# A graph network on one core: scores, value products and logits side by side, V copied by VectorE, loads reordered, last softmax by thirds

## The reference, cut to what matters

```
h   = relu(layernorm(x))                          # before M, and again before G
q,k,v = h@Wq+bq, h@Wk+bk, h@Wv+bv                 # 6 heads of 64
p   = softmax(q k^T / 8 + (0 where adj, else -9e15))
x1  = x + (p v)@Wf + bf                           # M and its residual

h   = relu(layernorm(x1))
hw  = h@W (12 heads of 32);  t = tanh(hw)
z   = leaky(t.w_src + (t.w_dst)^T), -999 where there is no edge
f   = elu(softmax(z) @ hw + b)
g   = sigmoid(h@H_w^T + H_b)
x2  = x1 + g*f + (1-g)*h                          # G and its residual
```

## Time and profile before

| | us |
|---|---|
| median of 3 runs | 2048.41 (2048.01 to 2048.42) |
| the profiled execution's own time | 2048.47 |
| its span in the profile | 2046.4 |
| PE busy in the span | 1979.5 (97%) |
| ACT busy | 1953.5 (95%) |
| DVE busy | 1813.4 (89%) |
| POOL busy | 1629.2 (80%) |
| mean granted clock of TensorE | 0.988 |

### The profile page before, as it was taken

How to read it: one execution, slowest core, us unless ns; L and a number is a source line. 1 busy time by engine, 2 the same in 40 slices (tenths; PEclk the granted TensorE clock), 3 DMA queues, 4 the chain that set the end, 5 groups by cost and what they waited for, 6 DMA issues and landing times.

```text
span 2046.4 us, 58352 instructions
## 1 busy us (share of the span) xinstructions
PE 1979.5 (97%) x19596; PEld 1845.0 (90%) x19596; DVE 1813.4 (89%) x4117; ACT 1953.5 (95%) x6800; POOL 1629.2 (80%) x2859
## 2 busy tenths in 40 slices
PE   4999999999999999999999999999999999999983
PEld 4899999999999999999999999999999999999972
DVE  4689999999999999999999999999999999999884
ACT  3799999999999999999999999999999999999995
POOL 3478888888888888888888888878888878888864
PEclk9999999999999999999999999999999999999995
DMA  5012223323323222223432222222222222221122
GB/s 170 12 46 67 70 60 79 86 68 91 86 65 83 53 51 57 56 50 82 122 99 58 53 52 60 50 53 61 50 52 61 50 54 60 50 52 49 39 47 50
DMA packets 309330, 130.62 MB, mean 64 GB/s; under 512 B 229547, under 2 KB 308782, under 8 KB 309038
## 3 DMA queue, kind: packets, MB, share of 16 engines
q1 hardware_dynamic: 309038, 126.90, 24.8%
HBM read 69.42 MB, written 57.41 MB: 62 GB/s over the span
## 4 chain that ended last, share of the span: by engine, by line
ACT 49%; DVE 37%; PE 5%; issue 4%; POOL 2%; DMA 1%; DVEq 1%; SPq 1%; POOLq 0%
ACT LG L506 27%; ACT LA L500 14%; DVE LG L636 11%; DVE neg_max L640 10%; DVE LA L613 9%; DVE stats L617 3%; ACT cT_hi L558 2%; ACT QKT L514 2%; ACT v L566 2%; PE psum L731 2%; DVE rdenG L632 1%; DVE rden L611 1%; ACT sdT L572 1%; PE psum L741 1%; DMA xin<-x 1%
## 5 line engine op out<-in xcount | busy, mean ns | idle before, releaser
L506 ACT ACTIVATE LG<-LG,neg_max 128x128 f32<-128x128 f32 x1536 | 595.4, 392 | 15.9 <-DVE neg_max L640 8.8
L500 ACT ACTIVATE LA<-LA,neg_max 128x128 f32<-128x128 f32 x768 | 297.9, 400 | 0.0
L506 ACT ACTIVATION_READ_ACCUMULATOR LG<-LG,neg_max 128x1 f32 x1536 | 291.9, 190 | 0.0
L430 POOL TENSOR_TENSOR prod<-th,vec 128x384 f32<-128x384 f32 x256 | 254.3, 1017 | 6.9 <-ACT th L543 6.9
L636 DVE COPY_PREDICATED_SCALAR LG<-no_edge,no_edge_score 128x1536 f32 x128 | 245.5, 1918 | 7.4 <-ACT LG L525 7.3
L640 DVE TENSOR_REDUCE neg_max<-LG 128x12 f32<-128x1536 f32 x128 | 224.4, 1753 | 13.8
L741 PE MATMUL psum<-hT_hi,qk_hi 128*128 128x256 f32 x1152 | 212.4, 292 | 8.5 <-DVE hT_lo L655 8.5
L613 DVE TENSOR_TENSOR LA<-LA,rden 128x768 f32<-128x768 f32 x128 | 199.0, 1555 | 4.4
L741 PE MATMUL psum<-hT_hi,qk_lo 128*128 128x256 f32 x1152 | 200.8, 282 | 0.0
L741 PE MATMUL psum<-hT_lo,qk_hi 128*128 128x256 f32 x1152 | 200.6, 282 | 0.0
L525 ACT ACTIVATE LG<-psum 128x1536 f32<-128x1536 f32 x128 | 186.4, 1457 | 2.3 <-PE psum L814 2.3
(11 more groups left out here) (121 smaller groups left out, 6201.5 us busy)
## 6 DMA issues: line engine op xcount, KB each, us to landing
context<-gcT SPq DMA_DIRECT2D x512, 48.0 KB, 2.1
back<-context SPq DMA_DIRECT2D x128, 192.0 KB, 2.5
xin<-x SPq DMA_DIRECT2D x64, 192.0 KB, 2.4
x_mid<-x SPq DMA_DIRECT2D x64, 192.0 KB, 2.4
xin<-x_mid SPq DMA_DIRECT2D x64, 192.0 KB, 2.4
out<-x SPq DMA_DIRECT2D x64, 192.0 KB, 2.3
ahead<-stage SPq DMA_DIRECT2D x16, 288.0 KB, 3.5
stage<-w_qk SPq DMA_DIRECT2D x12, 192.0 KB, 3.6
```

The lines of the kernel that those rows point to most:

```text
L430: last = pool.tensor_tensor(prod[:, i, :], th[:], vec[:, r.pair(k - 2), 2 + i, :], ALU.mult)
L500: last = act.activation(head, head, ACT.Exp, scale=-1.0, bias=neg_max[:, 0, h:h + 1], accum_out=rsum[:, h:h + 1])
L506: last = act.activation(head, head, ACT.Exp, bias=neg_max[:, 1, a:a + 1], accum_out=den[:, a:a + 1])
```

## The change

- PE's order in a step becomes: queries and keys (one third), V, LA transposes, LG transposes 0-3 and 8-11, sdT, LG 4-7, then scores, value products, logits, graph value products, then bias row, gate, h, hM and hG transposes, queries and keys (two thirds), O. Banks are dealt out anew.
- DVE copies V (`tensor_copy`), not ACT. ACT, DVE and POOL have new orders too, and other offsets between engines and graphs: steps run over k = -3 .. 136, and POOL, for one, does the gate layernorm for graph k-4 where it was k-1.
- The first pieces of the weights come in another order (`PIECES`), pieces 9 to 14, the graphs 4 to 7 and others are issued from the steps (`LOAD_STEP`), the splits move (`SPLIT_STEPS`), the bias setup too. POOL's `setup(-2)` for hb_row stays at -2, the first step with POOL work.
- The last graph's prelu, mask and maximum are done in three parts of four heads each; the exponentials of a part wait for that part's maximum. ACT's exponentials now stand as heads 8-11 at the end of a step and 0-3 and 4-7 in the next.
- SP: context, stores and loads at other offsets, the adjacency load last in a step.

The diff, cut to its core (of PE's order the new one, without the lines that it replaces):

```diff
-FIRST_STEP, STEPS_BEHIND = -7, 5
+FIRST_STEP, STEPS_BEHIND = -3, 9
...
-        PIECES = [("c00", 0, QK_ORDER[0] * 128, 128), ("c02", 0, QK_ORDER[2] * 128, 128),
-                  ("c01", 0, QK_ORDER[1] * 128, 128), ("c10", 0, QK_ORDER[3] * 128, 128),
-                  ("c12", 0, QK_ORDER[5] * 128, 128), ("c11", 0, QK_ORDER[4] * 128, 128),
+        PIECES = [("c01", 0, QK_ORDER[1] * 128, 128), ("c00", 0, QK_ORDER[0] * 128, 128),
+                  ("c02", 0, QK_ORDER[2] * 128, 128), ("c11", 0, QK_ORDER[4] * 128, 128),
                   ("V", 1, 0, COLS), ("V", 1, COLS, COLS),
+                  ("c10", 0, QK_ORDER[3] * 128, 128), ("c12", 0, QK_ORDER[5] * 128, 128),
                   ("O", 1, D, COLS), ("O", 1, D + COLS, COLS),
                   ("gate", 2, D, COLS), ("gate", 2, D + COLS, COLS),
                   ("h", 2, 0, COLS), ("h", 2, COLS, COLS)]
         READY = {name: n + 1 for n, (name, _, _, _) in enumerate(PIECES)}
-        SPLIT_STEPS = {-4: range(0, 3), -3: range(3, 6), -2: range(6, 8), -1: range(8, 11), 0: range(11, 14)}
+        LOAD_STEP = [-1, -1, -1, 0, 0, 0]
+        SPLIT_STEPS = {-2: range(0, 3), -1: range(3, 6), 0: range(6, 8), 1: range(8, 11), 2: range(11, 14)}
...
-        sdT_ps = psum[0:ROWS, 7, 512 - N:512].bitcast(BF16).rearrange("p (i n) -> p i n", i=2)
+        sdT_ps = psum[0:ROWS, 3, 512 - N:512].bitcast(BF16).rearrange("p (i n) -> p i n", i=2)
...
+                for m in range(8, len(PIECES)):
+                    if k == LOAD_STEP[m - 8]:
+                        load_piece(m)
+                for i in range(4, SLOTS):
+                    if k == max(i + -4, -1):
+                        load_x(x, i, i)
+                if k == 1:
+                    load_adj(HALF_SLOTS, 1)
+                    sp.dma_start(wf_stage[1], w_vf[1][:, D:2 * D].rearrange("(c p) n -> p c n", p=128)).then_inc(s["wf_in1"], 16)
+                    sp.dma_start(vec[:, 1, :, :], vecs[1].partition_broadcast(128)).then_inc(s["vec_in1"], 16)
...
                 if k == -2:
                     pool.wait_ge(s["hb_in"], 16)
                     head_bias()
-                if k == -1:
+                if k == 3:
...
+                if r.has(k - 6):
+                    if k - 6 < ALL - 1:
+                        act.wait_ge(s["z_max"], r.done(k - 6))
+                    else:
+                        act.wait_ge(s["last_max0"], 1)
+                    graph_exps(range(0, 4)).then_inc(s["z_exp0"], 1)
...
+                if r.has(k - 5):
+                    act.wait_ge(s["z_ps"], r.done(k - 5))
+                    if k - 5 < ALL - 1:
+                        act.activation(LG[:].rearrange("p (e n) -> p e n", e=3), banks(0, 3), ACT.Prelu, alpha=SLOPE).then_inc(s["z_leaky"], 1)
+                    else:
+                        for q in range(QUADS):
+                            act.activation(LG[:, q * 4 * N:(q + 1) * 4 * N], bank(0 + q), ACT.Prelu, alpha=SLOPE).then_inc(s["z_leaky" if q == QUADS - 1 else f"last_leaky{q}"], 1)
...
-                    act.wait_ge(s["z_max"], r.done(k - 3))
+                    if k - 5 < ALL - 1:
+                        act.wait_ge(s["z_max"], r.done(k - 5))
+                    else:
+                        act.wait_ge(s["last_max2"], 1)
                     graph_exps(range(8, 12)).then_inc(s["z_exp2"], 1)
...
+                        dve.wait_ge(s["masks"], r.done(k - 6))
+                        dve.copy_predicated(LG_heads, no_edge[:, (k - 6) % 2, :].unsqueeze(1).broadcast_to([128, GH, N]),
+                                            no_edge_score[:].unsqueeze(2).broadcast_to([128, GH, N])).then_inc(s["z_masked"], 1)
+                        dve.wait_ge(s["z_masked"], r.done(k - 6))
+                        dve.wait_ge(s["z_masked"], r.done(k - 6))
+                        dve.tensor_reduce(neg_max[:, 1, :], LG_heads, AX.X, ALU.max, negate=True).then_inc(s["z_max"], 1)
+                    else:
+                        dve.wait_ge(s["masks"], r.done(k - 6))
+                        for q in range(QUADS):
+                            heads = slice(4 * q, 4 * q + 4)
+                            if q == QUADS - 1:
+                                dve.wait_ge(s["z_leaky"], ALL)
+                            else:
+                                dve.wait_ge(s[f"last_leaky{q}"], 1)
+                            dve.copy_predicated(LG_heads[:, heads, :], no_edge[:, (k - 6) % 2, :].unsqueeze(1).broadcast_to([128, 4, N]),
+                                                no_edge_score[:].unsqueeze(2).broadcast_to([128, 4, N])).then_inc(s["last_masked"], 1)
+                            dve.wait_ge(s["last_masked"], q + 1)
+                            dve.tensor_reduce(neg_max[:, 1, heads], LG_heads[:, heads, :], AX.X, ALU.max, negate=True).then_inc(s[f"last_max{q}"], 1)
...
+                    dve.wait_ge(s["m_v"], r.done(k))
+                    dve.tensor_copy(v[:, (k) % 4, :], bank(2)[:, 0:D]).then_inc(s["m_val"], 1)
...
+                if r.has(k - 1):
+                    if (k - 1) % 2 == 0:
+                        for i in range(3):
+                            pe.wait_ge(s[f"qk{i}"], r.done(k))
+                    wait_latest(pe, r, ("g_lo", k - 4), ("s_max", k - 2))
+                    wait_latest(pe, r, ("g_haug", k - 5), ("s_max", k - 2))
+                    for h in range(MH):
+                        i = place_of(h)
+                        rows = slice(64 * (h % 2), 64 * (h % 2) + 64)
+                        at = slice((k - 1) % 4 * N, ((k - 1) % 4 + 1) * N)
+                        last = pe.matmul(bank(6 + i // KC)[:, (i % KC) * N:(i % KC + 1) * N],
+                                         QKT[rows, h // 2, at], QKT[rows, KC + h // 2, at], start=True, stop=True)
+                    last.then_inc(s["s_ps"], 1)
+                if r.has(k - 2):
+                    pe.wait_ge(s["pt"], r.done(k - 2))
+                    pe.wait_ge(s["m_val"], r.done(k - 2))
+                    wait_latest(pe, r, ("pt", k - 2), ("qk2", k), ("cT_lo", k - 3))
                     for h in range(MH):
                         i = place_of(h)
                         for e in range(2):
                             rows = slice(h % 2 * MD + e * GD, h % 2 * MD + (e + 1) * GD)
+                            last = pe.matmul(bank(5)[rows, h // 2 * N:(h // 2 + 1) * N], v[:, (k - 2) % 4, h * MD + e * GD:h * MD + (e + 1) * GD],
                                              PTA[:, i * N:(i + 1) * N], start=True, stop=True)
                     last.then_inc(s["c_ps"], 1)
+                if r.has(k - 5):
+                    pe.wait_ge(s["g_sdR"], r.done(k - 5))
+                    wait_latest(pe, r, ("gpt2", k - 6), ("x1", k - 3), ("z_leaky", k - 6))
+                    wait_latest(pe, r, ("gpt0", k - 6), ("m_lo", k + 2), ("z_leaky", k - 6))
+                    wait_latest(pe, r, ("gpt1", k - 6), ("m_val", k), ("qk0", k), ("z_leaky", k - 6))
                     for q in range(QUADS):
                         rows = slice(q * GROUP, (q + 1) * GROUP)
+                        last = pe.matmul(bank(0 + q), sdT[rows, (k - 5) % 2, :], sdR[rows, (k - 5) % 2, :, :].rearrange("p a n -> p (a n)"), start=True, stop=True)
                     last.then_inc(s["z_ps"], 1)
...
+                if r.has(k - 6):
+                    pe.wait_ge(s["gpt0"], r.done(k - 6))
+                    pe.wait_ge(s["gpt1"], r.done(k - 6))
+                    pe.wait_ge(s["gpt2"], r.done(k - 6))
+                    pe.wait_ge(s["g_haug"], r.done(k - 6))
+                    wait_latest(pe, r, ("g_sdR", k - 5), ("gc", k - 7))
                     for a in range(GH):
                         rows = slice(a % 4 * GD, (a % 4 + 1) * GD)
+                        last = pe.matmul(bank(3)[rows, a // 4 * N:(a // 4 + 1) * N], hv[:, (k - 6) % 2, a * GD:(a + 1) * GD],
                                          PTG[:, a // 4, (a % 4) * N:(a % 4 + 1) * N], start=True, stop=True)
                     last.then_inc(s["gc_ps"], 1)
+                if r.has(k - 4):
+                    weights("gate", k - 4)
+                    pe.wait_ge(s["g_lo"], r.done(k - 4))
+                    wait_latest(pe, r, ("pt", k - 2), ("qk1", k + 1), ("g_gate", k - 5))
+                    pe.matmul(bank(4)[:, 0:D], ones[ROWS:128, :], hb3[ROWS:128, r.pair(k - 4), :], start=True, stop=False)
+                    nodes_times(bank(4)[:, 0:D], g_hi, g_lo, hg_hi, hg_lo, D, begun=True).then_inc(s["g_gate_ps"], 1)
```

More of the change, by code:

```diff
@@ L398, in step @@
             def step(r, k):
[L399 to L406, removed]
@@ L417, in step @@
-                if r.has(k - 4):
-                    pool.wait_ge(s["g_gate"], r.done(k - 4))
-                    pool.tensor_scalar(gate[:, (k - 4) % HELD, :], gate[:, (k - 4) % HELD, :], 0.5, 0.5, ALU.mult, ALU.add).then_inc(s["g_sigmoid"], 1)
+                split_ahead(k)
+                if r.has(k - 6):
+                    pool.wait_ge(s["g_th"], r.done(k - 6))
+                    for i in range(2):
```

(30 more changed lines are left out.)

518 lines of the change are left out of this document (225 added, 293 removed).

## The result

The changed kernel takes 2077.13 us (median of 4 runs, 2075.77 to 2077.97) where the one before, run beside it, takes 2048.21 (2047.48 to 2048.42). The ratio is 1.0141, 95% interval 1.013 to 1.0153: slower, by 29 us. The prediction was 2074, with the right sign and, in the main, the right cause.

The account below looks back on a forecast made before the run. PE's full step was taken to bound the kernel: 2048.4 us, plus 0.20 x 122 steps = 24.4, plus 1.3 (-2 early steps, -1 filling, +5 draining, -0.7 last graph), gives 2074 us; range 2062 to 2088, 8 in 10 within 2039 to 2093.

Parts of the forecast that it names:

- PE's sum sets the pace: Steady middle: PE has no gap, so its step of 15.28 us is the period; the change makes it 15.48.
- rival (b): Steady middle: DVE becomes the bound, its waits exceeding its room; 15.63 us a step, 2092 us; chance 0.13.
- Changes of shape inside the tiled run: PE's tiled run: going between two tiled shapes costs as much as to or from the full array, 0.10 to 0.11 us.
- lone bias row: PE, behind the graph value products: bias row loses its cover beside the logits; its 384 columns cost 0.16 us alone.
- (a): PE's tiled run: shape changes inside it are free; net -0.14 us a step, 2033 us; chance 0.18.
- (c): PE's tiled run: new shape changes cost 0.05 us each, net about 0.02 a step, 2052 us; chance 0.09.
- Net per step: PE's steady step: 0.50 us new less 0.30 gone, net +0.20, over 122 steps +24.4 us.
- Filling: Start: POOL's hb_row wait delays the first query product to about 27.0 us; first graph value product earlier, net -1 us.
- Draining: After the last query product: first of six outstanding logit products comes later, against thinner steps; +5 us, bounds -3 and +12.
- the one that I said would stay: Draining loop: gate product waits for the logits before it, and these for th, prod, sd and its parts on POOL.
- Thirds: Last graph: prelu, mask and maximum in thirds gain two thirds of the prelu less four instruction starts, -0.7 us.
- DVE's room, 0.65 less 0.5: DVE's steady step: 14.83 us of work leaves 0.65 us under 15.48; a 0.5 us wait for hT_hi fits.

Follow-up runs that it names:

- Experiment 5: Kernel before, with V copied by DVE instead of ACT, between the second y and sdR: 2048.7 us, ratio 0.9999.
- Experiment 1: Changed kernel with graph value products ahead of the logits in PE's order, the bias row beside the logits: 2033.6 us, ratio 0.9923.
- experiment 2: Changed kernel with only the gate's bias row moved from behind the graph value products to beside the logits: 2046.8 us, ratio 0.9992.
- experiment 4: Changed kernel with POOL's wait for hb_row moved from step -2 to step 0: 2069.7 us, ratio 1.0107.
- experiment 6: Changed kernel without the last graph's split, prelu, mask and maximum of all twelve heads at once: 2075.82 us (one run).
- experiment 7: Changed kernel with the last graph's exponentials in the order of their maxima, heads 0-3, 4-7, 8-11: 2075.34 us (one run).
- experiment 3: Kernel before, with V copied by DVE instead of ACT, behind gT_lo and ahead of hv and y: 2121.09 us, ratio 1.035.

## Why the prediction was right

- **PE's sum sets the pace: right.** Experiment 5 shows it for the kernel before, experiments 1 and 2 for the changed one, whose period follows PE's order to the hundredth. In its middle PE waited for nobody; rival (b) did not come about. DVE's wait for hT_hi is there in 37 of 96 steps.
- **Changes of shape inside the tiled run: right.** Value products to logits cost 0.11 (0.11 predicted), logits to graph value products and those to the bias row 0.11 each and 0.02 for the slow start. The lone bias row costs 0.16 of columns. Rivals (a) and (c) fall. Experiment 1 does land at (a)'s numbers, 15.10 and 2033.6 against 15.14 and 2033, but by avoiding the changes that (a) took to be free; the likeness is chance.
- **Net per step: 0.20 predicted, 0.227 measured** (15.507 - 15.280). The rest, 0.03, is the V product. Behind the tiled run its later trios ran at 0.52 (1208.26 to 1208.78); behind queries and keys they take 0.53 (1212.58 to 1213.11).
- **A term that was missing: the second half of the profiled execution.** There the 18 gate and h matmuls take 3.284 us instead of 3.227 (trios 0.53 apart, 1204.46 to 1204.99, where experiment 1 shows 0.52), and the period is 15.560. Over 60 steps that is 3.2 us. It starts behind an irregular step (15.65) where pair 1 takes over. Pair 1's weights and instructions alone don't bring it about: the profiled executions of experiments 4, 6 and 7, with the same steady order, ran at 15.507 in both halves. What puts an execution into one or the other stays open, and so does how many of the four timed executions had it.
- **The middle as a sum:** 120 steps of 0.227 are 27.2 and the second half 3.2. What the kernel before lost over 15.28 in its steps, 2.3 in all, is gone (predicted 2, for the early steps alone). Together +28.1, measured +26.1. The other -2.1 is where the stretch ends: the last query product now stands 6.5 us behind the last graph value products before it, where it was 8.6.
- **Filling: right mechanism, sized wrongly.** POOL's wait for hb_row stood where predicted, but the data came 0.9 us earlier than in the kernel before (16.14 against 17.06), the five operations took 1.3 instead of 1.7, and the first query product started at 25.53 rather than 27.0. The first graph value product gained 3.8 us, not 1.
- **Draining: right size, wrong loop.** +6.6 against +4.3 (5 less 0.7). Of the 6.6, 2.1 is the other side of the -2.1 above; counted from those graph value products it is +4.5 (94.2 instead of 89.7). The granted clock over it is the same, 0.85 and 0.84. The waits at the end name another loop than the one that I said would stay: PE waits for the exponentials of LG, 19.7 us in 6 waits, and the next logits then wait 0.78 us for ACT's copy of the transposed LG, whose bank they overwrite. Logits, prelu, mask, maximum, exponentials, transposes, copy, logits: with z behind the LG transposes in PE's order, one graph must be through before the next begins. This is read from the waits; no run tested it.
- **Thirds: right reason, smaller.** 0.2 instead of 0.7. ACT's order began with the last maximum, as argued; experiment 7 mended that and ran into DVE's order.
- **DVE's room, 0.65 less 0.5:** held, but the reasoning was unsafe. The sum and one walk through the order didn't show the loop over POOL that experiment 3 met. In the changed kernel the copy still stands between sd and y:

```profile
1211.52 0.91 DVE L668 TENSOR_REDUCE sd<-prod 128x24 f32<-128x768 f32 x1
...
1214.53 0.55 DVE L687 COPY v<-psum 128x384 f32<-128x384 f32 x1
```

  What has room there is POOL's new order: prod is over at 1209.88, 1.6 us before sd begins, and x follows the end of y by 0.8. The prediction didn't look at either.

In sum the parts were off by +2.8 (the steady steps), +3.2 (second half) and +2.3 (draining) against -2.1 (its other side), -0.3 (steps over 15.28) and -2.8 (filling), which with the +0.1 at the end makes 28.9 of the predicted 25.7, against 29.1 measured. The main term was right by its mechanism. That the total missed by only 3 is in part luck, as filling's miss took away most of the second half's. The stated range is also narrower than its own bounds give: net 0.13 with -3 for draining comes to 2058, and 0.28 with +12 to 2091.

## What to carry to other kernels

Count the changes of tile shape in an order written by hand, inside a tiled run as well as at its edges, and put blocks of like shape together, with a narrow matmul beside one that leaves its strip free: swapping two blocks was worth 44 us here. Where a busy engine sets the period, work taken from another brings nothing, and work given to a third is free only in a gap that no loop passes through. Believe of the chain of waits that its loop is long, not that the others are short: look for every wait that comes back in each step.

## What the runs showed of the hardware that was not expected

The same fp32 products of 384 columns run at either of two pitches, 0.52 or 0.53 us for three, with the granted clock at 1.00 in both. Which one goes with what stands ahead: the V product shows 0.52 behind the tiled run and 0.53 behind queries and keys. For the gate and h products it also goes with the execution: in the profiled one of the changed kernel it changed once, at an irregular step near 1040 us, and held for 900 us. Repeated runs of one kernel spread by 2 to 6 us, and this pitch alone moves 3 of them.
